# Self attention in eight tiles: exponentials group by group on ScalarE, and a tile's rounding inside the next tile's softmax

## The reference

```python
q  = fp8_linear(ln(x), wq);  k, v = fp8_linear(...)      # 16 heads in 8 groups, width 128, each normalised
p  = softmax(q @ k.T / sqrt(128))                        # over 64 keys, per sequence and head
core = p @ v                                             # self attention
cross = the same with 1601 context rows
y  = fp8_round(concat(core, cross) / smooth)             # clamp, round to fp8, then the output projection
x  = x + y @ wproj
```

## Time and profile before

| what | value |
|---|---|
| median of 3 runs | 2562.75 us |
| profiled execution | 2561.66 us, span 2559.8 us, mean granted TensorE clock 0.94 |
| busy over the span | PE 2266.5 (89%), DVE 1937.3 (76%), ACT 1561.3 (61%), POOL 1405.7 (55%) |
| tile 0 to tile 5 of the self attention, from one first maximum to the next | 45.06, 36.06, 37.31, 37.42, 36.98, 35.58 us |
| tile 6 | 30.00 us |
| start of tile 0, start of tile 7 | 99.24 and 357.65 us |

### The profile page before, as it was taken

One profiled execution on the slowest core, in us unless ns is written; L12 is line 12 of the kernel. 1 busy time (PEld: TensorE's weight loads), 2 busy tenths in 40 slices (PEclk: granted clock), 3 DMA queues, 4 the chain that ended last, 5 costly groups with the idle time before them and its releaser, 6 DMA issues. The chain is left out here.

```text
span 2559.8 us, 49662 instructions
## 1 busy us (share of the span) xinstructions
PE 2266.5 (89%) x18258; PEld 1853.3 (72%) x18258; DVE 1937.3 (76%) x4402; ACT 1561.3 (61%) x3135; POOL 1405.7 (55%) x1537
## 2 busy tenths in 40 slices
PE   3868867999999999999999999999999999584666
PEld 1545656888888888888888888888888887362334
DVE  8988866777877777787777778777877877478753
ACT  5666645676777677677767767776776676211211
POOL 4334347776667677666767766676776655050000
PEclk8778879999999999999999999999999999786788
DMA  3112111101110111111011111101111000362100
GB/s 115 59 51 76 50 70 48 41 34 48 35 35 32 43 37 34 48 35 35 29 47 37 34 47 36 35 27 48 37 34 41 17 2 1 123 232 53 37 13 8
DMA packets 74478, 119.40 MB, mean 47 GB/s; under 512 B 21168, under 2 KB 56576, under 8 KB 73216
## 3 DMA queue, kind: packets, MB, share of 16 engines
q1 hardware_dynamic: 74240, 116.23, 13.4%
HBM read 94.20 MB, written 22.02 MB: 45 GB/s over the span
## 5 line engine op out<-in xcount | busy, mean ns | idle before, releaser
L75 PE MATMUL x_kc<-x_wk,x_ctxT 128*128 128x256 f16 x4992 | 623.3, 274 | 11.3 <-ACT x_sq L911 11.3
L75 PE MATMUL x_ox<-x_ctxp,x_pt 128*128 128x256 f16 x4992 | 609.6, 273 | 0.0
L681 POOL TENSOR_SCALAR x_kT<-x_kf 128x512 f16<-128x512 f32 (+1 forms) x448 | 282.2, 630 | 502.8 <-ACT x_kf L919 502.6
L75 PEld LDWEIGHTS x_kc<-x_wk,x_ctxT 128*128 128x128 f16 x4992 | 489.8, 98 | 82.7 <-ACT x_sq L911 14.5
L75 PEld LDWEIGHTS x_ox<-x_ctxp,x_pt 128*128 128x128 f16 x4992 | 484.3, 98 | 52.8
L683 POOL TENSOR_TENSOR x_kT<-x_kf,x_kT 128x512 f16<-128x512 f32 (+1 forms) x448 | 492.1, 1098 | 37.5
L1376 DVE TENSOR_TENSOR x_pt<-x_tp,x_pt 128x512 f16<-128x512 f32 (+1 forms) x512 | 288.9, 585 | 221.9 <-ACT x_pt L948 221.9
L1319 DVE TENSOR_REDUCE x_ss<-x_sq 128x4 f32<-128x512 f32 (+1 forms) x448 | 283.1, 644 | 170.1 <-ACT x_sq L911 169.6
L919 ACT ACTIVATE x_kf<-x_tp,x_hv 128x512 f32<-128x512 f32 (+1 forms) x448 | 331.8, 759 | 113.5 <-PE x_tp L1089 113.5
L907 ACT ACTIVATE x_kraw<-x_kc 128x512 f32<-128x512 f32 (+1 forms) x448 | 255.1, 569 | 150.8 <-PE x_kc L75 146.5
L948 ACT ACTIVATE x_pt<-x_tp 128x512 f16<-128x512 f32 (+1 forms) x512 | 259.3, 520 | 72.8 <-PE x_tp L1129 68.7
(11 more groups left out here) (246 smaller groups left out, 3048.4 us busy)
## 6 DMA issues: line engine op xcount, KB each, us to landing
x_stage<-in_ctxT SPq DMA_DIRECT2D x32, 800.5 KB, 4.4
x_stage<-in_ctx SPq DMA_DIRECT2D x16, 896.0 KB, 5.1
x_stage<-in_ctx SPq DMA_DIRECT2D x16, 640.0 KB
scr_q<-a_qxT SPq DMA_DIRECT2D x8, 1024.0 KB, 3.9
x_qs<-scr_q SPq DMA_DIRECT2D x16, 512.0 KB, 5.3
scr_core<-a_catc SPq DMA_DIRECT2D x8, 512.0 KB, 2.6
scr_x<-x_catx SPq DMA_DIRECT2D x8, 512.0 KB, 2.9
f_area<-in_wprojT SPq DMA_DIRECT2D x4, 1024.0 KB, 10.9
```

What stands on the lines that cost most here:

```text
L75: last = pe.matmul(out, lhs[i], rhs[j], start=start and n == 0, stop=stop and n == len(parts) - 1)
L681: gp.tensor_scalar(dst[0], src, 1.0, 0.0, ALU.mult, ALU.add).then_inc(khi_ready, 1)
```

## The change

The maximum is multiplied by minus the scale of the softmax on DVE, into mx. ACT then computes, for each of the 16 blocks, one exponential of 128 x 64 directly from PSUM, with that value as its bias, and has the sum over the 64 keys accumulated into the new tile `sums`. DVE's subtraction and sum go. The bank of the scores is free after the exponentials (exp_ready), not after the subtraction.

The rounding of tile t-1's outputs is done in tile t (for t from 1 to 6): its three short steps between the maxima and the first reciprocal, its addition behind the probabilities. Tile 6 also rounds its own outputs behind them; tile 7's rounding stays where it was. `keep_core` on POOL and `store_core` on SP move by a tile accordingly.

```diff
@@ buffers, semaphores, the bank of the scores
+        sums = sb("sums", [P, 2 * G])
-        sub_ready = sem("sub_ready")
+        max_ready = sem("max_ready")
-            sem_, value = {"s": (sub_ready, t * 2), "t": (turned, (t + 1) * HU), "p": (pt_ready, t * 4),
+            sem_, value = {"s": (exp_ready, t * 2), "t": (turned, (t + 1) * HU), "p": (pt_ready, t * 4),
@@ SyncE
             for t in range(0, TILES - 1):
                 store_q(t + 1)
-                store_core(t)
+                if t:
+                    store_core(t - 1)
...
+            store_core(TILES - 2)
@@ GpSimd
             split_queries(1)
-            keep_core(0)
             for t in range(1, TILES - 1):
...
                 if 2 <= t < 4:
-                    gp.wait_ge(sub_ready, 2 * t + 2)
+                    gp.wait_ge(max_ready, 2 * t + 2)
...
                 if t == TILES - 2:
-                    gp.wait_ge(sub_ready, 2 * t + 2)
+                    gp.wait_ge(max_ready, 2 * t + 2)
                     gp.wait_ge(raw_ready, TILES * HU)
-                    gp.wait_ge(core_ready, t)
+                    gp.wait_ge(core_ready, t - 1)
...
-                keep_core(t)
+                keep_core(t - 1)
+            keep_core(TILES - 2)
@@ ScalarE
             def exps(t, j):
-                act.wait_ge(sub_ready, t * 2 + j + 1)
-                act.activation(sm[:, 8 * j:8 * j + 8, :], sm[:, 8 * j:8 * j + 8, :], ACT.Exp,
-                               scale=SOFTMAX_SCALE).then_inc(exp_ready, 1)
+                act.wait_ge(max_ready, t * 2 + j + 1)
+                for i in range(8 * j, 8 * j + 8):
+                    src = tr[:, bank_of(("s", j)), (i - 8 * j) * S:(i - 8 * j + 1) * S]
+                    ins = act.activation(sm[:, i, :], src, ACT.Exp, bias=mx[:, i:i + 1], scale=SOFTMAX_SCALE,
+                                         accum_out=sums[:, i:i + 1])
+                ins.then_inc(exp_ready, 1)
@@ VectorE
+            def rounding_steps(c, at, kept, count):
                 c.done(v.tensor_scalar(yb[:, at], ys[:, at], FP8_MAX, -FP8_MAX, ALU.min, ALU.max))
                 c.done(v.tensor_scalar(eb[:, at], yb[:, at].bitcast(U16), 0x7F80, None, ALU.bitwise_and))
+                if count:
+                    v.wait_ge(kept, count)
                 c.done(v.tensor_scalar(yf[:, at], eb[:, at].bitcast(BF16), FP8_MIN_NORMAL, FP8_ROUND, ALU.max, ALU.mult))
-                return v.tensor_tensor(mg[:, at], yf[:, at], yb[:, at], ALU.add)
@@ attend, first half
                     c.done(v.tensor_reduce(mx[:, 8 * j:8 * j + 8], src, X, ALU.max))
-                    v.tensor_tensor(sm[:, 8 * j:8 * j + 8, :], src, mx[:, 8 * j:8 * j + 8].unsqueeze(2).to_broadcast([P, 8, S]),
-                                    ALU.subtract).then_inc(sub_ready, 1)
+                    v.tensor_scalar(mx[:, 8 * j:8 * j + 8], mx[:, 8 * j:8 * j + 8], -SOFTMAX_SCALE, None, ALU.mult
+                                    ).then_inc(max_ready, 1)
+                if 0 < t < TILES - 1:
+                    rounding_steps(c, slice(0, 2048), core_ready, t - 1)
...
                     v.wait_ge(exp_ready, t * 2 + j + 1)
-                    e = sm[:, 8 * j:8 * j + 8, :]
-                    c.done(v.tensor_reduce(mx[:, 8 * j:8 * j + 8], e, X, ALU.add))
-                    c.done(v.reciprocal(mx[:, 8 * j:8 * j + 8], mx[:, 8 * j:8 * j + 8]))
+                    c.done(v.reciprocal(sums[:, 8 * j:8 * j + 8], sums[:, 8 * j:8 * j + 8]))
...
+                if 0 < t < TILES - 1:
+                    v.tensor_tensor(mg[:], yf[:], yb[:], ALU.add).then_inc(core_rounded, 1)
@@ attend, behind the outputs
-                if t < TILES - 1:
+                if t == TILES - 2:
                     v.wait_ge(y_ready, t * 4 + 4)
-                    quantise(c, 0, 2048).then_inc(core_rounded, 1)
+                    rounding_steps(c, slice(0, 2048), core_ready, t)
+                    v.tensor_tensor(mg[:], yf[:], yb[:], ALU.add).then_inc(core_rounded, 1)
```

More of the change, by code:

```diff
@@ L277, in attend_self_and_cross @@
                      ("t", 6), ("t", 7), ("e", 4), ("e", 5), ("e", 6), ("e", 7), ("t", 8), ("t", 9), ("e", 8), ("e", 9)]
-        ATTEND_OPS = 9
-        DVE_PER_TILE = ATTEND_OPS + 16
         def weights(part, k, lo, hi):
@@ L1231, in _ @@
             c.done(v.reciprocal(smooth[:], smooth[:]))
-            def quantise(c, at, n, kept=None):
-                at = slice(at, at + n)
+            def rounding_steps(c, at, kept, count):
                 c.done(v.tensor_scalar(yb[:, at], ys[:, at], FP8_MAX, -FP8_MAX, ALU.min, ALU.max))
                 c.done(v.tensor_scalar(eb[:, at], yb[:, at].bitcast(U16), 0x7F80, None, ALU.bitwise_and))
-                if kept is not None:
-                    v.wait_ge(xq_ready, kept)
+                if count:
+                    v.wait_ge(kept, count)
                 c.done(v.tensor_scalar(yf[:, at], eb[:, at].bitcast(BF16), FP8_MIN_NORMAL, FP8_ROUND, ALU.max, ALU.mult))
-                return v.tensor_tensor(mg[:, at], yf[:, at], yb[:, at], ALU.add)
             def low_weights(n0, n1):
@@ L1257, in rounding @@
                     v.wait_ge(y_scaled, KC * m + k + 1)
-                    quantise(c, k * T, T, KC * (m - 1) + k + 1 if m else None).then_inc(mg_ready, 1)
+                    at = slice(k * T, k * T + T)
+                    rounding_steps(c, at, xq_ready, KC * (m - 1) + k + 1 if m else 0)
+                    v.tensor_tensor(mg[:, at], yf[:, at], yb[:, at], ALU.add).then_inc(mg_ready, 1)
             low_weights(0, 2)
@@ L1445, in attend @@
                                               sm[:, 8 * j + b:8 * j + 8:2, :],
-                                              mx[:, 8 * j + b:8 * j + 8:2].unsqueeze(2).to_broadcast([P, 4, S]), ALU.mult)
+                                              sums[:, 8 * j + b:8 * j + 8:2].unsqueeze(2).to_broadcast([P, 4, S]), ALU.mult)
                     ins.then_inc(probs_ready, 1)
+                if 0 < t < TILES - 1:
+                    v.tensor_tensor(mg[:], yf[:], yb[:], ALU.add).then_inc(core_rounded, 1)
                 if t + 2 < TILES:
@@ L1455, in attend @@
                     normalise_keys(0, 1)
-                if not (isinstance(t, int) and t == 0):
-                    v.wait_ge(core_ready, t)
-                    v.sem_inc(passed_dve, 1)
                 for j in range(4):
@@ L1477, in _ @@
             normalise(1, c, range(HU))
+            c = Chain(v, dve, 0, 0)
             def tile(t, more):
-                c = Chain(v, dve, DVE_PER_TILE, t)
                 attend(t, c)
@@ L1485, in tile @@
                     normalise(t + 2, c, range(4, HU))
-                    c.end()
             tile(0, True)
@@ L1490, in _ @@
                 tile(t, True)
[L1492 to L1495, removed]
+            tile(TILES - 2, False)
+            tile(TILES - 1, False)
             v.wait_ge(y_ready, TILES * 4)
+            v.wait_ge(core_ready, TILES - 1)
             c.done(v.tensor_scalar(yb[:], ys[:], FP8_MAX, -FP8_MAX, ALU.min, ALU.max))
```

## The result

| | before | after |
|---|---|---|
| median | 2561.8 us (20 runs, 2560.0 to 2563.2) | 2557.4 us (20 runs, 2552.0 to 2559.7) |
| ratio, 95% interval | | 0.9983 [0.9977, 0.9989] |
| profiled execution, span | 2561.66, 2559.8 us | 2555.71, 2553.9 us |
| tiles 0 to 5 | 45.06, 36.06, 37.31, 37.42, 36.98, 35.58 | 37.69, 35.06, 36.08, 35.12, 35.04, 35.86 |
| tile 6; tile 7 to the first transposition of the cross attention | 30.00; 22.87 | 34.86; 22.67 |

The changed kernel's time lies inside the wide range of the forecast (2556 to 2583 us), outside the range of its own case (2563 to 2576), and on the other side of "no change". In the profiled executions the first transposition of the cross attention comes 8.86 us earlier (371.66 against 380.52). Of that, 3.0 us are given back behind it, and the span is 5.9 us shorter.

A forecast was written before the change was run, and what follows sets the result against it. DVE's chain and the PE and ACT chain meet in each tile's last statistics, the latter with 1.3 us slack. Terms -4.7 + 3.7 + 0.2 + 3.6 + 3.5 = +6.3: 2569 us median, range 2563 to 2576, wide 2556 to 2583.

The forecast's parts named there:

- its own case: Whole kernel: the forecast's main case, 2568 us profiled and 2569 median, range 2563 to 2576, chance 0.57.
- DVE's new waits: Profile after: DVE would newly stand idle before the statistics of the projection units behind the outputs.
- ACT's chain as what sets e2: Tiles 1 to 5: longer exponentials on ACT start projection unit 2 later by 2.46 us, 1.5 in tiles 2 and 3.
- pair: ACT's softmax: one 128x64 exponential with its sum's read-out takes 0.33 us, sixteen 5.28 us per tile.
- Tile 0: First tile: no rounding of its own and no POOL difference beside the weights' centring, outputs +2.46: -4.7 us.
- Tiles 1 to 5: Tiles 1, 4 and 5 +1.13 us each, 2 and 3 +0.15 each, together +3.7; 0.1 per tile added for contention.
- Tile 6: Two roundings: exponentials' 3.13 us reach the outputs whole, and 0.5 for POOL's difference: +3.6 us.
- Tile 7: Exponentials delay keys, root and probabilities by 4.14 us, less the 0.68 sum DVE no longer takes: +3.5 us.
- (a): TensorE's clock rises ahead of projection unit 2 in six tiles, with pairs of 0.30 us: -5.4, 2557 us; chance 0.18.
- (b): TensorE's clock rises later, so projection units 2 and 3 and the first outputs run at half: +13, 2582; chance 0.12.
- (c): Exponential and read-out pairs on ACT do not overlap in a row of sixteen: +33, 2602 us; chance 0.06.
- (d): Numbers hold but waits in ACT and PE absorb them, tile 0's gain balancing the rest: +1, 2564 us; chance 0.07.

The follow-up runs named there:

- e3: Not a run here: projection unit 3 on TensorE, in each tile of the self attention; with unit 2 it took 2.93 us before and 1.89 after in tile 1.
- e4: Changed kernel with each block of the second half of the scores in two exponentials of 32 columns, second sum left out of the divisor: 2568.1 us, ratio 1.0027.
- e1: Changed kernel with the rounding and storing back behind each tile's own outputs, only the new exponentials with their sums left: 2568.1 us, ratio 1.0027.
- e12: The kernel of e6 without read-outs on ScalarE's sixteen exponentials, the sums back on VectorE: 2549.8 us, ratio 0.9956.
- e5: Kernel before, old softmax, with the whole rounding behind the next tile's probabilities and tile 6's sums of squares ahead of the roundings: 2551.6 us, ratio 0.9959.
- e8: The kernel of e5 with 8 overwritten matmuls of 128x512 per tile in tiles 1 to 5 to keep TensorE busy: 2559.0 us, ratio 0.9988.
- e6: Changed kernel with tile 6's last three sums of squares of the keys ahead of that tile's own rounding on VectorE: 2546.7 us, ratio 0.9939.

## Why the prediction was wrong

**The structure held.** What it said of DVE's new waits, of tile 0 without its rounding, of the stretch from outputs to spread (11.27 us; 11.32 measured) and of ACT's chain as what sets e2 is in the trace. One reading was loose: of DVE's 4.6 idle us in tile 1 before, 3.00 are the wait that it names and 0.17 stand before the outputs; the rest are pieces too small for a row. With the clock held equal, five tiles cost 0.96 us more, where the forecast had 3.9 and the shorter pair takes 3.2 off it (5 x 16 x 0.04).

**The step that failed** is that e2 and e3, and the p2 ahead of them, keep their durations. It took the clock of before for the clock of after. By tile 1: the outputs were forecast at T + 16.2 and stood at T + 14.01. Of these 2.2 us, about 0.6 are the pair (16 x 0.04), 0.56 lie between p2's start and e2's (1.17 us, not 1.73), and 1.04 are e2 and e3 (1.89, not 2.93). The two clock terms are 1.6 us. The tile is 1.0 shorter, not 1.13 longer, and with the pair they are the whole miss in it, to 0.1 us.

**Term by term.** Tile 0: -7.4, not -4.7; the outputs are not late at all (T + 14.00, before T + 14.06), by the same terms. Tiles 1 to 5: -6.2, not +3.9; clock 7.2, pair about 3. Tile 6: +4.9, not +3.6 (+4.1 with the squares first): the outputs are 1.8 us late, not 3.1, but the rounding of tile 6 lasts 9.0 us beside GpSimd's difference for tile 5 (a step of 2.50 and a wait of 2.08, above) where it took 4.9, and the forecast gave 0.5 to that. Tile 7: -0.2, not +3.5. The exponentials did arrive there (PE waits 10.63 us for the probabilities, 7.65 before), but scores, keys and value units ran at full clock, 2.06 + 1.47 + 1.89 us, where they had taken 3.83 + 2.77 + 2.00: 3.2 us less, nearly all of it inside the tile. Behind the self attention +3.0 us, which the forecast had not. The scores of tile 7, before and after:

```profile
357.19 3.83 PE L1041 MATMUL a_tr<-a_kT,a_qT 128*128 128x64 f32 x17
```

```profile
348.68 2.06 PE L1045 MATMUL a_tr<-a_kT,a_qT 128*128 128x64 f32 x17
```

**The rivals.** (a) forecast 2557 and the mechanism that happened, an earlier rise and a shorter pair, and it had 0.18. That its sum meets the time so closely is in part luck: by its terms, tiles 0 to 5 came out 2.0 us better, and tiles 6 and 7 with what follows 1.6 worse. The argument against it was that the new gaps are no shorter. The gaps ahead of t2 and t3 are indeed longer (3.75 and 1.23 us, against 0.84 and 0.67), but from t3 to e2 PE has one gap of 0.33 us, where before it had 1.06 and 0.81 in the same tile:

```profile
145.76 0.66 PE L1036 MATMUL a_tr<-a_ident,a_raw 128*128 128x128 f32 x4 [0.84 <-DVE a_sm L1431]
147.09 0.66 PE L1036 MATMUL a_tr<-a_ident,a_raw 128*128 128x128 f32 x4 [0.67 <-DVE a_sm L1431]
148.81 1.94 PE L1046 MATMUL a_tr<-a_ident,a_pp 128*128 128x128 f32 x8 [1.06 <-DVE a_pp L1444]
```

The new ACT chain holds t3 back until the first probabilities are nearly ready, so the pieces close up. That could be worked out from the forecast's own times, t3's and p0's, and was not. The condition that rival (a) set, e2 before about T + 10, was wrong too (e4). (b), (c) and (d) did not occur.

**What stays open** is what fixes the moment of the rise. In the changed kernel, in e1 and in e4 the clock rose ahead of e2 or early enough within it that e2 and e3 took 1.89 to 2.48 us; before, they took 2.43 to 3.62. The denser train goes with the earlier rise, but tiles 1 and 5 of e12 have the same train from t3 on and different clocks, so the train just ahead of e2 does not fix it alone. The moment of the fall is a rival that no run tests. Windows of tile 1 before and after, then of tiles 1 and 5 of e12, cut where the granted clock changes:

```profile
148.55:155.38 6.83, 5.77 (x21) 4.00 (x22) 4.34 (x13) 5.30 (x10) 6.50 (x8) 0.50 0.00 0
```

```profile
139.41:146.24 6.83, 4.05 (x17) 3.26 (x18) 5.49 (x9) 6.83 (x30) 2.49 (x2) 0.50 0.00 0
```

```profile
139.92:150.16 10.24, 8.52 (x30) 5.59 (x31) 9.95 (x22) 7.60 (x17) 8.31 (x8) 0.50 0.00 1
283.27:290.10 6.83, 4.16 (x16) 3.00 (x16) 6.55 (x14) 6.83 (x23) 2.27 (x3) 0.50 0.01 2
```

In tile 1 the low stretch is as long in both kernels. It ends 1.8 us earlier in the changed one because it begins 1.8 us earlier (T + 2.44, not T + 4.25), while PE stands idle ahead of t2. In e12 the clock falls at T + 0.73 in tile 5 and at T + 3.61 in tile 1. In other tiles the length differs too: the rise stood at T + 11.1, 12.6, 12.8, 12.9 and 10.1 in tiles 1 to 5 before, and stands at T + 9.3, 11.8, 9.8, 8.8 and 11.3 in the changed kernel. That the clock was up earlier ahead of e2, and what it gave, is shown; why it rose earlier is not.

## What to carry to other kernels

In a stage where TensorE waits often, take no duration of its instructions over from before without asking at which clock it was measured; price the sum at both clocks and let the range hold both. Two edits that are each a loss can be a gain together when one makes the wait that the other fills: test the parts and the whole. And where engines work in order, look at what stands behind a long instruction that nobody waits for: three sums of squares moved ahead of one rounding were worth 8 to 11 us, more than the change.

## What the runs showed of the hardware

- Adding 40 matmuls of 128x512 in five tiles made the kernel before 7.8 us faster; adding them to e5's kernel, whose next wait is for DVE (e8), made it 7.4 us slower.
- An exponential of 128x64 from PSUM with a pointer bias costs 0.20 us in a row (e12, 3.31 us for sixteen) and 0.29 with its read-out. The estimate of 0.35 us without read-out, from the Trainium skill, "ScalarE: Activation LUTs", Rules for kernel authors, was too high for a row of them: one lasts 0.30 us (138.12), and the next starts before it ends. The measurement decides.
- DVE's scaling of 128x8 took 0.17 us alone, and 1.60 us in tile 7 of e6, beside GpSimd's difference; its sums of 128x512 in tile 2 of e12 stayed at 0.67 to 0.69 us beside GpSimd's conversions, while the multiplications between them rose from 0.76 to 1.35 and 1.78 us for two. The Trainium skill, "SBUF — State Buffer", Who interferes with whom, has reductions free of this contention, and these rows agree.
